# A decoder kernel on one core: a program of its own for preparing the first batch element

## What is computed

```python
x = _layernorm(x + self_attention(x))        # 16 heads of 8, causal, window 64, relative bias
x = _layernorm(x + cross_attention(x, ctx))  # 16 heads of 64; keys rotated by cos and sin
x = _layernorm(x + ternary_ffn(x))
x = _layernorm(x + recurrence(x))            # 256 steps of tanh(state @ A.T + u @ B.T) + sp
x = _layernorm(x + linear_attention(x, ctx)) # needs layernorm(ctx @ wk), layernorm(ctx @ wv)
x = _layernorm(x + fp8_ffn(x))
```

## Time and profile before

| | us |
|---|---|
| median of 3 runs | 1079.42 (1076.92 to 1081.24) |
| profiled execution | 1080.22 |
| its span, first to last instruction | 1078.5 |
| PE busy | 932.1 (86%) |
| DVE, ACT, POOL busy | 686.1 (64%), 513.8 (48%), 503.9 (47%) |
| first instruction of the batch loop (PE L1906) | at 88.65 |

### The profile page before, as it was taken

How to read it: one execution, slowest core, us unless ns; L and a number is a source line. 1 busy time by engine, 2 the same in 40 slices (tenths; PEclk the granted TensorE clock), 3 DMA queues, 4 the chain that set the end, 5 groups by cost and what they waited for, 6 DMA issues and landing times.

```text
span 1078.5 us, 22081 instructions
## 1 busy us (share of the span) xinstructions
PE 932.1 (86%) x8504; PEld 660.6 (61%) x8504; DVE 686.1 (64%) x1905; ACT 513.8 (48%) x1446; POOL 503.9 (47%) x637
## 2 busy tenths in 40 slices
PE   3658998999899899989999998999989589999932
PEld 2436665666666666666656665666656379888721
DVE  3355657767776765777577658757689634444467
ACT  3645563565466456536645663564334023333324
POOL 1034356536644653565465456446567211333354
PEclk9989899999999999999999999999999669999955
DMA  7100000000000000000000000000000001222211
GB/s 180 28 1 6 11 1 2 5 12 1 6 11 1 2 6 11 1 7 11 2 1 6 11 2 1 1 2 1 21 1 1 1 7 25 32 33 32 32 12 40
DMA packets 60422, 15.09 MB, mean 14 GB/s; under 512 B 41230, under 2 KB 59678, under 8 KB 60190
## 3 DMA queue, kind: packets, MB, share of 16 engines
q1 hardware_dynamic: 60318, 13.69, 6.0%
HBM read 10.51 MB, written 3.17 MB: 13 GB/s over the span
## 4 chain that ended last, share of the span: by engine, by line
PE 63%; DVE 18%; ACT 7%; POOL 5%; issue 3%; DMA 2%; SPq 2%; POOLq 0%; DVEq 0%
PE score_banks L1906 9%; PE out_bank L1830 8%; PE score_banks L1637 5%; PE bank_a L1618 5%; DVE o_rec L1238 4%; PE score_banks L1844 4%; PE score_banks L1662 3%; DVE prob L1336 3%; PE bank_d L1713 3%; PE score_banks L1639 3%; PE score_banks L1638 3%; PE score_banks L2034 3%; PE out_bank L1813 2%; PE out_bank L1838 2%; PE bank_d L2047 2%
## 5 line engine op out<-in xcount | busy, mean ns | idle before, releaser
L914 ACT ACTIVATE prob<-score_banks 128x1024 f32<-128x1024 f32 x128 | 131.2, 1025 | 165.1 <-PE score_banks L1906 164.8
L694 POOL TENSOR_TENSOR psum<-psum,prob 128x512 f32<-128x512 f32 x64 | 81.7, 1276 | 155.0 <-DVE prob L1336 154.9
L1906 PE MATMUL score_banks<-qh,kr 64*128 64x256 f32 x1024 | 150.1, 413 | 1.7 <-ACT qh L873 1.3
L1238 DVE RECIPROCAL o_rec<-out_bank 128x256 f32<-128x256 f32 x64 | 111.9, 1748 | 26.2 <-PE out_bank L1838 26.2
L692 POOL TENSOR_TENSOR psum<-prob 128x512 f32<-128x512 f32 x64 | 82.9, 1295 | 95.2 <-DVE prob L1336 95.0
L1830 PE MATMUL out_bank<-prob,v 128*64 128x256 f32 x1024 | 124.6, 385 | 1.4 <-DVE on L1239 1.4
L1906 PEld LDWEIGHTS score_banks<-qh,kr 64*128 64x128 f32 x1024 | 91.2, 191 | 40.5 <-issue 30.9
L845 ACT ACTIVATE prob<-prob,neg_max 128x128 f32<-128x128 f32 (+1 forms) x256 | 107.0, 426 | 12.9 <-DVE neg_max L1138 12.9
L1336 DVE TENSOR_SCALAR prob<-prob 128x1024 f32<-128x1024 f32 x128 | 100.5, 785 | 12.9 <-ACT prob L914 12.9
L1830 PEld LDWEIGHTS out_bank<-prob,v 128*64 128x64 f32 x1024 | 67.8, 136 | 46.6 <-issue 17.2
L963 ACT ACTIVATE prob<-score_banks 128x8 f32<-128x8 f32 x255 | 45.3, 178 | 97.5 <-PE score_banks L2034 97.5
(11 more groups left out here) (384 smaller groups left out, 2115.4 us busy)
## 6 DMA issues: line engine op xcount, KB each, us to landing
cb<-in_ctx_dram SPq DMA_DIRECT2D x8, 256.0 KB, 2.9
bias_mask<-bias_scratch SPq DMA_DIRECT2D x1, 1536.0 KB, 7.3
xb<-in_x_dram SPq DMA_DIRECT2D x8, 128.0 KB, 2.1
prob<-in_L_xattn_Wkv_dram SPq DMA_DIRECT2D x1, 1024.0 KB, 7.2
x_scratch<-v SPq DMA_DIRECT2D x16, 64.0 KB, 1.5
bias_mask<-x_scratch SPq DMA_DIRECT2D x16, 64.0 KB
att_scratch<-on SPq DMA_DIRECT2D x16, 64.0 KB, 1.5
prob<-att_scratch SPq DMA_DIRECT2D x16, 64.0 KB, 3.0
```

Source lines behind the costliest of these rows:

```text
L914: s.activation(prob[:, p % 2, 2 * u:2 * u + 2, :].rearrange("p k (h q) -> p h k q", h=2), sc[:, 0:2, :].rearrange("p h (k q) -> p h k q", ...
L1238: link(w.reciprocal(o_rec[:, :], bank[:, T:2 * T]))
L1906: last = mm(sc[:, h, k * T:(k + 1) * T], kr[rows_of, p % 2, kb * P:(kb + 1) * P], qh[rows_of, p % 2, :], start=True, stop=True, skip_group ...
```

## The change

SP's order of loads is new: relative bias, `x`, projections, context, then the rest; they have semaphores of their own (`rel_in`, `qkv_in`, `split_in`, `keep_in`, `bias_in[0..3]`). The bias is read back in four parts, one for each group of heads. Every engine has a written-out program for element 0 in place of the loop over 48 slots. Score stages use in turn `bank_d`/`bank_d2` and two of the score banks; turns of probabilities use in turn `bank_a`, copied by ACT, and `out_bank`, copied by DVE. The context products use `bank_p`. ACT writes the high parts of the weights one at a time between its exponentials, POOL writes the low parts. ACT's first instruction is now a small copy of `head_mask`. After the attention, keys and values of the cross attention are computed while the norms run, in `bank_p` and `bank_d2` by turns, and queries last. From the loop on, the code is the same, but for counts of semaphores and one wait of PE in element 1 (`FIRST_DONE`).

```diff
-FIRST_JOBS = {("keys a", 0): 0, ("keys b", 0): 0, ("queries", 0): 0, ("values 0", 0): 0, ("values 1", 0): 0,
-              ("keys a", 1): 1, ("keys b", 1): 1}
+FIRST_JOBS = {("keys a", 0): 0, ("keys b", 0): 0, ("values 0", 0): 0, ("values 1", 0): 0, ("keys a", 1): 1,
+              ("keys b", 1): 1, ("queries", 0): 0}
...
     for (kind, k), target in FIRST_JOBS.items():
-        add((kind, k), kind, target, "o0")
+        add((kind, k), kind, target, "d2")
...
+            load(rel, a["L0_attn_rel_bias"][MAX_REL:MAX_REL + WINDOW + 1, :], signal=rel_in)
+            sp.dma_start(xb[:, :, :], a["x"][0].rearrange("(k p) d -> p k d", p=P)).then_inc(x_in, 16)
+            load(w_nat[:, 0:3, :], a["L0_attn_w_qkv"].rearrange("(k p) c -> p k c", p=P), signal=qkv_in)
+            load(w_nat[:, 3, :], a["L0_attn_w_proj"], signal=qkv_in)
+            sp.dma_start(cb[:, :, :], a["ctx_1024"][0].rearrange("(k p) d -> p k d", p=P)).then_inc(ctx_in, 16)
...
+            sp.wait_ge(d_free, 1)
+            sp.dma_start(scratch, rel_row).then_inc(scratch_out, 16)
...
+            load(keep[:, :, :], a["mask_BxS2_ff1"].rearrange("b (k p) -> p b k", p=P), slow=True, signal=keep_in)
+            sp.wait_ge(scratch_out, 16)
+            for j in range(G):
+                sp.dma_start(bias_mask[:, j:H:G, :], rows(scratch, (1, P), j * SCRATCH, [(G * SCRATCH, G), (1, BAND)])
+                             ).then_inc(bias_in[j], 16)
+            load(wkv_nat, a["L0_xattn_Wkv"], signal=split_in)
+            load(wq_nat, a["L0_xattn_Wq"], signal=split_in)
...
+            def split_low(part, low, full, high):
+                pool.wait_ge(weights_high, part + 1)
+                return g.tensor_tensor(low, full, high.bitcast(F32), ALU.subtract)
 
             pool.wait_ge(first_in, 16 * FIRST_LOADS)
-            for slot in range(SLOTS):
+            for slot in (S_X, S_CTX, S_KV_SCALE[0]):
                 self_attention(0, slot, 0, after=False)
-            rotate(0)
+            swapped = "c (h t d) -> c t h d"
+            split_low(0, wk_s[:, 1, :], wkv_nat[:, 0:INNER], wk_s[:, 0, :])
+            for t in range(2):
+                high, low = (wkx_s[:, k, :].rearrange(swapped, t=2, d=HALF)[:, t] for k in range(2))
+                split_low(1, low, wkv_nat[:, 0:INNER].rearrange(swapped, t=2, d=HALF)[:, 1 - t], high)
+            self_attention(0, S_KV_SCALE[1], 0)
+            split_low(2, wq_s[:, 1, :], wq_nat, wq_s[:, 0, :])
+            split_low(3, wv_s[:, 1, :], wkv_nat[:, INNER:2 * INNER], wv_s[:, 0, :]).then_inc(weights_split, 1)
+            for slot in (*S_AFFINE, S_PROJ, S_X1):
+                self_attention(0, slot, 0)
             rotate(1)
...
+            exps_of(0, 0, 0, 1)
+            keep_kv(0, 0)
+            exps_of(0, 1, 0, 2)
+            even_turn(0)
+            exps_of(0, 1, 1, 2)
+            even_turn(2)
+            split_high(0)
+            exps_of(0, 2, 0, 2)
+            even_turn(4)
+            exps_of(0, 2, 1, 2)
+            split_high(1)
+            exps_of(0, 3, 0, 2)
+            even_turn(6)
+            exps_of(0, 3, 1, 2)
+            keep_kv(0, 1)
+            even_turn(8)
+            split_high(2)
+            even_turn(10)
+            split_high(3)
+            first_job(FIRST_REC, rec_t[:, :], bank_a[:, 0:T])
...
+            for slot in (S_CTX, S_Q, S_V):
                 self_attention(0, slot, 0)
...
+            prepare_trig()
+            centre_weights()
+            keep_cos()
+            dve.wait_ge(scratch_out, 16)
+            w.memset(prob1[:, :, 0:WINDOW], 0.0)
+            measure_kv(0, 0)
+            for at in range(6):
+                first_score(at)
+            odd_turn(1)
...
+            pe.wait_ge(weights_split, 1)
+            pe.wait_ge(cn_split, 1)
+            pe.wait_ge(kv_free, 2)
+            prep_keys(JOB["keys a", 0], 0, "a")
+            self_attention(0, S_PROJ)
+            prep_keys(JOB["keys b", 0], 0, "b")
+            for half in range(2):
+                prep_values(JOB[f"values {half}", 0], 0, half)
+            prep_keys(JOB["keys a", 1], 0, "a")
+            prep_keys(JOB["keys b", 1], 0, "b")
+            pe.wait_ge(weights_in, 16 * SETUP_LOADS)
+            pe.wait_ge(lat_ready, 1)
...
+            prep_queries(JOB["queries", 0], 0)
+            self_attention(0, S_KV_SUM)
```

More of the change, by code:

```diff
@@ new lines, in _ @@
+            for jj in HEAD_PAIRS:
+                s.activation(km[:, jj, :], k0[:, :], ACT.Identity, scale=mask_of_8[:, jj:jj + 1]).then_inc(km_ready, 1)
+            act.wait_ge(ctx_full, 1)
+            s.activation(ctx_t[:, :], bank_p[:, :], ACT.Identity).then_inc(ctx_kept, 1)
+            act.wait_ge(trig_full, 2)
+            s.activation(sin_t[:, :], sc[:, 1, :], ACT.Identity, scale=sign[:, 0:1]).then_inc(sin_kept, 1)
+            apply_norm(0).then_inc(cn_ready, 1)
+            act.wait_ge(ctx_cols_in, 16 * 2)
@@ L1217, in _, with odd_turn @@
[L1217 to L1227 removed]
+            def odd_turn(at):
+                dve.wait_ge(odd_full, at // 2 + 1)
+                w.tensor_copy(pt[:, 1, :], ob[:, :]).then_inc(odd_free, 1)
@@ new lines, in _ @@
+            pe.wait_ge(qkv_in, 16 * 2)
+            for k in range(4):
+                last = turn(bank_d2[:, k * P:(k + 1) * P], w_nat[:, k, :])
+            last.then_inc(d_full, 1)
+            pe.wait_ge(d_free, 2)
+            pe.wait_ge(a_free, FIRST_X)
+            mm(bank_a[:, 0:T], w_qkv_t[:, D:2 * D], x_t[:, :], start=True, stop=True).then_inc(a_full, 1)
+            self_attention(0, S_Q)
+            self_attention(0, S_V)
+            pe.wait_ge(ctx_in, 16)
+            for k in range(KB):
+                last = turn(bank_p[:, k * P:(k + 1) * P], cb[:, k, :])
@@ new lines, in first_weigh @@
+            def first_weigh(t):
+                if t % 2 == 0:
+                    pe.wait_ge(a_free, FIRST_TURN + t // 2)
+                else:
+                    pe.wait_ge(odd_free, t // 2 + 1)
+                return weigh_turned(t)
+            first_scores(0)
+            pe.wait_ge(kv_centred, 1)
+            pe.wait_ge(ctx_kept, 1)
+            products_of_ctx(0, bank_p)
+            first_scores(1)
+            pe.wait_ge(cn_ready, 1)
+            for k in range(KB):
+                last = turn(ob[:, k * P:(k + 1) * P], cn[:, k, :])
@@ new lines, in _ @@
+            last.then_inc(cn_full, 1)
+            for at in range(2, 6):
+                first_scores(at)
+            first_turn(0)
+            first_turn(1)
+            first_scores(6)
+            first_weigh(0)
+            first_turn(2)
+            first_scores(7)
+            first_weigh(1)
+            pe.wait_ge(kv_free, 1)
+            products_of_ctx(1, bank_p)
+            for at in range(3, TURNS):
+                first_turn(at)
+                first_weigh(at - 1)
+            pe.wait_ge(rec0_ready, 1)
@@ new lines, in _ @@
+            prep_keys(JOB["keys a", 0], 0, "a")
+            self_attention(0, S_PROJ)
+            prep_keys(JOB["keys b", 0], 0, "b")
+            for half in range(2):
+                prep_values(JOB[f"values {half}", 0], 0, half)
[3 more added lines that the diff above has]
+            pe.wait_ge(lat_ready, 1)
+            for qt in range(QT):
+                last = turn(bank_a[:, qt * P:(qt + 1) * P], lat[:, qt, :])
```

417 lines of the change are left out of this document (247 added, 170 removed).

## The result

The changed kernel takes **1047.82 us** (median of 4 runs, 1047.52 to 1049.39), the kernel before 1079.44 beside it (1076.92 to 1081.24): a ratio of 0.9719, 95% interval 0.9698 to 0.9741. One later execution of the changed kernel, at a mean granted clock of 0.571, took 1420.08 us and is left out of every figure here.

A forecast was written before the change was run, and what follows sets the result against it. A chain of waits ahead of the PE-bound batch loop sets the gain: 15.9 + 7.9 + 0.9 give 24.65 us; 1080.2 - 24.65 = 1055.5, less 0.8 is 1054.8, said as 1055. Range 1049 to 1062.

The forecast's parts named there:

- Part 1: Start to ACT's first exponential: 21.85 instead of 37.71 us, 15.9 earlier, range 15 to 17.
- from there the same work in the same lengths as before: From the key product at 7.7 us, work keeps its old lengths, giving the first context product's end at 18.0.
- the 0.7 us at worst: Bias there at 20.1 us against 19.4 when DVE asks; 0 if a quarter loads quicker than the whole.
- Part 2: First exponential to `rec_t`: ACT becomes the bound, 24.1 instead of 32.0 us, 7.9 earlier.
- Part 3: `rec_t` to the loop's first instruction on PE, 18.9 us before; loop forecast at 64.0, 0.9 of the gain.
- I take 64.0, nearer to the lower: Loop start, chosen between 64.8 with TensorE at its lower level and 61.5 at its upper.
- 5.2 us; before it was 8.5: Projection to `lat` ahead of the loop: 5.2 us forecast against 8.5 before, the gain being in the norms.
- Norms: Ahead of `lat`: with POOL's affines over earlier, DVE's two norms take 0.57 us instead of 1.53.
- stay low in part 2: Rival: TensorE at its lower level from first exponential to `rec_t`, `rec_t` some 5 us later, 1060; chance 0.13.
- POOL's splits: Rival: DVE's work stretches POOL's last two splits up to twice 2.55 us, loop 3 to 5 later, 1059; chance 0.10.
- Only the loads: Rival: only DVE's earlier start on the scores pays, 6.4 us, 1073; chance 0.05.
- Slower: Rival: TensorE's grant in the loop falls by 0.045 or more, costing 30 us, 1085; chance 0.03.

The follow-up runs named there:

- the repetition: The changed kernel run again unaltered, on one chip beside the kernel with DVE's split: 1048.1 us, ratio 0.9737.
- DVE's split: Against the changed kernel, keys wait only for their own low parts and DVE, not POOL, subtracts the last: 1045.86 us (0.9691), again 1050.69 (0.975).

## Why the prediction was right, and where it was off

- **Bound and shape: right.** The gain lies ahead of the loop, 30.75 of 32.6 us, and in the parts in which it was forecast. The remaining 1.9 us lie in the loop, 989.9 against 988.0, inside what identical loops differ by (986.3 in the repetition).
- **Part 1: right in mechanism, mis-sized by 3.4 us** (19.3, forecast 15.9, range 15 to 17). The step that failed is "from there the same work in the same lengths as before". `w_proj` and with it the key product were 0.7 early. From the first of the turns to the end of the context product it took 2.9 us instead of the 5.2 of my sum, and the reading behind it 0.4 less. In the repetition the same three took 1.97, 1.44 and 1.50, together 4.8, and the part gave 18.05. So TensorE's level is 1.8 of the 3.4; the rest is the earlier load (0.7 here, 1.3 there) and lengths that I had rounded up. I had both levels in the earlier trace rows, named them for one term only, the context product, and closed the range at 17.
- **The loads** were there in time, as said; the 0.7 us at worst came to 0. Their order matters through who reads them: 8 us in the changed kernel.
- **Part 2: right, 23.8 against 24.1.** ACT is the bound with two pairs of banks. I had given the second pair no price of its own; it is 7.1 us, 2.4 of them ahead of the first exponential, and about 4 of the 7.1 the alternation of PE and DVE.
- **Part 3: mis-sized by 2.3 us** (3.2, forecast 0.9; 15.7 us from `rec_t` to the loop, forecast 18.0, or 18.8 at the lower level). The table sets my sum at the lower level beside both traces:

  | us | sum | first trace | repetition |
  |---|---|---|---|
  | `rec_t` to the first keys | 2.8 | 2.56 | 2.56 |
  | keys ahead of the projection | 1.4 | 0.82 | 1.37 |
  | projection to the end of `lat` | 6.3 | 6.07 | 6.52 |
  | from there to the turn of `lat` | 3.3 | 2.49 | 2.69 |
  | turn of `lat` to the loop | 5.0 | 3.73 | 3.50 |

  The failed term is "I take 64.0, nearer to the lower". The keys took 0.8 at the upper level and the 1.4 of my sum at the lower. The queries and the sums, 2.9 in my sum, took 1.5 in both traces, at the upper level. The values and the keys of pair 1 were through 0.6 to 0.8 sooner than I had them, although pair 1's keys ran at the lower level in both (0.43 apart, against 0.24 for the first keys in the first trace); so that is no matter of level. With the upper one throughout my sum gave 61.5, that is 15.5 us from `rec_t`, and the first trace took 15.7 with a mixture of levels: near, but in part by chance.
- **Two slips in part 3's sum.** From 51.3 the terms add to 55.95, not 56.5. And "5.2 us; before it was 8.5" counts the one from the projection's end and the other from its start. From start to the end of `lat` it is 8.5 before, 6.3 in the forecast and 6.07 measured.
- **Norms: right**, 0.60 for two. In the row of 1.53 before, the first norm took 1.28 us, to 75.06, 0.1 behind the end of POOL's affine, and the second 0.34: one was held up, and the 75.3 that I set against the rule is the end of the second. A run with DVE's split beside POOL's second affine shows the same conflict from the other side (below).
- **Rivals.** TensorE did not stay low in part 2 of the changed kernel; it did for a stretch with one pair of banks, where the level's share is 0.8 to about 3 us, not the 5 that I gave it. POOL's splits were not stretched: 2.34 to 2.50 us. Only the loads: refuted. Slower: the grant from 400 to 500 us is 0.98, against 0.96.
- **Chances and range.** The range left out what the profile itself showed, that both levels occur in part 1. With the 1.8 us for it the lower end would have been near 1047, and the time inside.

## What to carry to other kernels

In a stretch where no engine is busy for long, price every TensorE product at both of its lengths and let the range span both; the same program may get either. A second pair of banks is worth the other engine's reading time per stage only as long as the stages stand ahead of the bound, so look at what follows the last stage, not at the shares. And before a wait is paid for or removed, name what is late right behind it: here the removal of a 2 us wait gave 0.1 at most.
